# DLRM tower: the first chunk's x rows made by transposes instead of a trip through DRAM

## What is computed

```python
e = stack([tbl_f[ids[:, f]] for f in range(32)], axis=1)     # (B=512, F=32, D=32) fp32
x0 = prev = e
for W in (filter_0, filter_1):                               # (F*32, 128), (F*128, 128)
    z = einsum('bhd,bmd->bhmd', x0, prev)                    # all products of a field and a previous row
    cur = relu(einsum('bpd,pn->bnd', z.reshape(B, -1, D), W))
    outs.append(cur); prev = cur
z = concatenate(outs, axis=1).sum(-1)                        # (B, 256)
h = relu(concatenate([z, dense_ctx], 1) @ W_top1 + b_top1)
h = relu(h @ W_top2 + b_top2)
y = h @ W_top3                                               # (B, 1)
```

## Time and profile before

| | us |
|---|---|
| median of 3 runs | 919.02 (917.8 to 921.05) |
| the profiled execution | 922.03 |
| its span | 920.0 |
| TensorE matmuls busy in the span | 840.2 (91%) |
| VectorE busy | 747.0 (81%) |
| ScalarE busy | 763.2 (83%) |
| GpSimd busy | 677.8 (74%) |

### The profile page before, as it was taken

How to read it: one execution, slowest core, us unless ns; L and a number is a source line. 1 busy time by engine, 2 the same in 40 slices (tenths; PEclk the granted TensorE clock), 3 DMA queues, 4 the chain that set the end, 5 groups by cost and what they waited for, 6 DMA issues and landing times.

```text
span 920.0 us, 14382 instructions
## 1 busy us (share of the span) xinstructions
PE 840.2 (91%) x3572; PEld 668.7 (73%) x3572; DVE 747.0 (81%) x2380; ACT 763.2 (83%) x2568; POOL 677.8 (74%) x650
## 2 busy tenths in 40 slices
PE   0316999999999999999999999999999999999988
PEld 0113787787888788887887888877888888888753
DVE  0223688898998988988998999988999999999891
ACT  1314999999999899999998999999999999999842
POOL 6772778888888898888888888876676666667550
PEclk9999999999999999999999999999999999999998
DMA  9144666666767666767766677667667766764430
GB/s 268 16 116 128 164 156 153 145 159 161 176 157 163 146 147 160 166 145 173 170 152 145 157 166 153 151 153 169 157 152 166 161 152 153 162 148 94 90 69 0
DMA packets 57718, 133.84 MB, mean 145 GB/s; under 512 B 8785, under 2 KB 22321, under 8 KB 57538
## 3 DMA queue, kind: packets, MB, share of 16 engines
q0 software_dynamic: 22528, 69.22, 41.4%
q1 hardware_dynamic: 32178, 59.94, 20.0%
q10 hardware_dynamic: 2928, 3.76, 1.4%
HBM read 62.64 MB, written 5.24 MB: 74 GB/s over the span
## 4 chain that ended last, share of the span: by engine, by line
PE 53%; DMA 13%; issue 10%; DVE 9%; POOL 9%; ACT 4%; another core or an unknown queue 1%; POOLq 0%; DVEq 0%; ACTq 0%
DMA scaled<-scaled 13%; PE ya L652 9%; PE ya L654 9%; PE ya L653 8%; PE yd L654 6%; PE yd L653 6%; PE yd L652 6%; DVE acc L574 5%; ACT scaled L444 3%; POOL quarter L314 3%; POOL quarter L310 2%; PE acc L652 2%; PE acc L654 2%; PE acc L653 2%; POOL part L318 2%
## 5 line engine op out<-in xcount | busy, mean ns | idle before, releaser
L444 ACT ACTIVATE scaled<-ya,emb 128x128 f32<-128x128 f32 x2304 | 659.7, 384 | 63.4 <-PE ya L654 55.7
L574 DVE SCALAR_TENSOR_TENSOR acc<-yd,emb,acc 128x128 f32<-128x128 f32 x1408 | 395.5, 343 | 7.5 <-PE yd L654 7.5
L310 POOL TENSOR_TENSOR quarter<-scaled 128x512 f32<-128x512 f32 x128 | 197.8, 1545 | 81.5 <-DMA scaled<-scaled 69.6
L652 PE MATMUL ya<-w_hi,prev_hi 128*128 128x512 f32 x576 | 227.3, 395 | 10.3 <-DVE prev_lo L540 5.5
L653 PE MATMUL ya<-w_lo,prev_hi 128*128 128x512 f32 x576 | 225.2, 391 | 0.0
L654 PE MATMUL ya<-w_hi,prev_lo 128*128 128x512 f32 x576 | 225.0, 391 | 0.0
L652 PE MATMUL yd<-w_hi,prev_hi 128*128 128x512 f32 x448 | 175.2, 391 | 1.8 <-DVE pooled_b L593 1.5
L654 PE MATMUL yd<-w_hi,prev_lo 128*128 128x512 f32 x448 | 174.4, 389 | 0.0
L653 PE MATMUL yd<-w_lo,prev_hi 128*128 128x512 f32 x448 | 174.4, 389 | 0.0
L303 POOL DMA_DIRECT2D scaled<-scaled x128 | 119.0, 930 | 73.6 <-ACT scaled L444 69.0
L287 POOL DMA_INDIRECT emb<-in_tbl,idx x128 | 132.8, 1038 | 30.3 <-issue 27.2
(11 more groups left out here) (68 smaller groups left out, 723.7 us busy)
## 6 DMA issues: line engine op xcount, KB each, us to landing
scaled<-scaled POOLq DMA_DIRECT2D x128, 512.0 KB
xb<-xt_scratch SPq DMA_DIRECT2D x64, 512.0 KB
x<-xt_scratch SPq DMA_DIRECT2D x64, 192.0 KB
xm<-xt_scratch SPq DMA_DIRECT2D x32, 256.0 KB
emb<-in_tbl,idx POOLq DMA_INDIRECT x128, 4.2
scaled<-in_L_rec_filter SPq DMA_DIRECT2D x8, 256.0 KB
xt_scratch<-xt_stage SPq DMA_DIRECT2D x7, 256.0 KB
xt_scratch<-xt_stage SPq DMA_DIRECT2D x9, 128.0 KB
```

The source lines that it names most:

```text
L310: pool.tensor_tensor(four, piece[:, 0:C], piece[:, C:2 * C], ALU.add).then_inc(quartered, 1)
L444: op = act.activation(scaled[:, tile % PR, C * j + N * i:C * j + N * (i + 1)], ya[:, n % RA, N * i:N * (i + 1)], ACT.Copy, scale=scale_of( ...
L574: dve.scalar_tensor_tensor(after, y_part, scale_of(tile, HB * j + i), before, ALU.mult, ALU.add).then_inc(chained, 1)
L652: pe.matmul(dst, v_hi, m_hi, start=start, stop=False)
```

## The change

For chunk 0 the loads from the scratch, the split products and the small product go. ScalarE repeats each field four times (repeat_four_times), VectorE lays the fields out in four steps (spread_up, nine copies). TensorE transposes these into PSUM: the x that everything is multiplied by, its rows once, and five sets of rows, 28 transposes in seven groups. ScalarE copies two of them to SBUF, VectorE makes five products, and TensorE multiplies them whole in fp32 with the unsplit filter (five matmuls), in place of 13 fp32r ones. Ahead of it stand 34 matmuls whose result is not used (WARM), behind the first 24 gathers. Loads begin at chunk 1; the first write takes columns of chunks 1 to 3, and the second write goes ahead of the first load. The steps of chunk 1's layer 0 move to later places in chunk 0 on ScalarE, TensorE and GpSimd, and EARLY_NEXT goes from 22 to 12. Waits that count chunks are shifted by one; those lines are left out here.

```diff
-    EARLY_NEXT = 22
+    EARLY_NEXT = 12
+    WARM = 34
...
+        fields_up = sb("fields_up", [P, DC, 4 * (F + 4)])
+        fields_four_times = sb("fields_four_times", [P, DC, 4 * F])
...
+        first_product = scaled_flat[:, (F + 2 * KT + 2) * N:(F + 2 * KT + 2) * N + (KT + 1) * C].rearrange(
+            "p (t c) -> p t c", t=KT + 1)
+        first_x = scaled_flat[:, 8192:8192 + C]
+        first_x_once = scaled_flat[0:F, 8192 + C:8192 + 2 * C]
...
+        first_rows = [yd[:, 0, :], yd[:, 1, :], yd[:, 2, :], prod[:], xm_ps[:]]
+        FIRST_TURN = (2, 4, 5, 6, 7)
...
+        def first_emb(fields):
+
+            return emb[:, 0, D * fields.start:D * fields.stop].rearrange("b (f d) -> b d f", d=D)[:, 0:DC]
...
             sp.wait_ge(a_used, 1)
-            write_xt(0, 0, 2, xt_first_written)
+            write_xt(0, 1, 4, xt_first_written)
+            sp.wait_ge(a_used, 2)
+            write_xt(0, 4, CPB)
             sp.wait_ge(xt_first_written, 32)
-            load_l0(0)
             load_l0(1)
-            sp.wait_ge(a_used, 2)
-            write_xt(0, 2, 4)
-            write_xt(0, 4, CPB)
-            sp.wait_ge(xt_written, 64)
-            for c in range(2, CHUNKS):
+            load_l0(2)
+            sp.wait_ge(xt_written, 32)
+            for c in range(3, CHUNKS):
...
-            small_product(1)
             for c in range(CHUNKS):
-                if c + 1 < CHUNKS:
+                if 0 < c < CHUNKS - 1:
...
-                    if q == 1 and c + 2 < CHUNKS:
+                    if c == 0 and q == 1:
+                        small_product(1)
+                    if c == 0 and q == 2:
+                        small_low(1)
+                    if c + 2 < CHUNKS and q == (3 if c == 0 else 1):
...
+            def repeat_four_times(fields):
+                once = first_emb(fields)
+                act.activation(fields_four_times[:, :, 4 * fields.start:4 * fields.stop].rearrange("b d (f i) -> b d f i", i=4),
+                               bass.AP(once.tensor, once.offset, [list(dim) for dim in once.ap] + [[0, 4]]),
+                               ACT.Copy).then_inc(four_times_ready, 1)
+
             act.wait_ge(gathered_first, 16 * EARLY)
+            repeat_four_times(slice(0, EARLY))
             sort_d(0, slice(0, EARLY))
             act.wait_ge(gathered[0], 16 * (F - EARLY))
+            repeat_four_times(slice(EARLY, F))
             sort_d(0, slice(EARLY, F))
+            act.wait_ge(first_turned, 1)
+            act.activation(first_x, xm_ps[:], ACT.Copy).then_inc(first_x_copied, 1)
+            act.wait_ge(first_turned, 3)
+            act.activation(first_x_once, acc0[0:F], ACT.Copy).then_inc(first_x_copied, 1)
             stage_xt(0, 0)
             stage_xt(0, 1)
-            copy_xm(0)
-            split_high(0, 0)
-            small_high(0)
-            for k in range(1, KT):
-                split_high(0, k)
             prev_high(0)
...
+                        if c == 0:
+                            if (q, j) == (1, 1):
                                 copy_xm(1)
-                            if j == 1:
+                            if (q, j) == (1, 3):
                                 split_high(1, 0)
-                            if j == 2:
+                            if (q, j) == (2, 0):
                                 split_high(1, 1)
-                            if j == 3:
+                            if (q, j) == (2, 1):
+                                split_high(1, 2)
+                            if (q, j) == (2, 2):
                                 small_high(1)
-                        elif j == 0 and (q < 3 and c + 1 < CHUNKS):
-                            split_high(c + 1, q + 1)
-                        if j == 0 and (q == 3 and c + 2 < CHUNKS):
-                            split_high(c + 2, 0)
-                        if (q, j) == (3, 1) and c + 1 < CHUNKS:
-                            prev_high(c + 1)
-                        if c + 2 < CHUNKS:
-                            if (q, j) == (2, 2):
-                                copy_xm(c + 2)
-                            if (q, j) == (3, 3):
-                                small_high(c + 2)
+                            if (q, j) == (2, 3):
+                                split_high(1, 3)
+                            if (q, j) == (3, 1):
+                                copy_xm(2)
+                            if (q, j) == (3, 2):
+                                split_high(2, 0)
+                            if (q, j) == (3, 4):
+                                prev_high(1)
+                                small_high(2)
...
+            def spread_up(i, fields, at):
+
+                dve.tensor_copy(fields_up[:, :, 4 * at + i:4 * (at + fields.stop - fields.start - 1) + i + 1:4],
+                                first_emb(fields)).then_inc(fields_up_ready, 1)
+
+            def spread_up_last():
+                n = F - EARLY
+                last = first_emb(slice(EARLY, F))
+                to = fields_up[:]
+                dve.tensor_copy(bass.AP(to.tensor, 4 * (EARLY - 12) + 3, [list(to.ap[0]), list(to.ap[1]), [15, 4], [4, n]]),
+                                bass.AP(last.tensor, last.offset, [list(last.ap[0]), list(last.ap[1]), [0, 4], list(last.ap[2])])
+                                ).then_inc(fields_up_ready, 1)
+
+            def multiply_first(t):
+                if t == 0:
+                    dve.wait_ge(first_x_copied, 1)
+                if t == KT:
+                    dve.wait_ge(first_x_copied, 2)
+                dve.wait_ge(first_turned, FIRST_TURN[t])
+                if t < KT:
+                    product = dve.tensor_tensor(first_product[:, t, :], first_rows[t], first_x, ALU.mult)
+                else:
+                    product = dve.tensor_tensor(first_product[0:F, t, :], first_rows[t][0:F], first_x_once, ALU.mult)
+                product.then_inc(first_multiplied, 1)
...
-            product(0, 0)
-            first_small()
-            for k in range(KT):
-                split_low(0, k)
-                if k + 1 < KT:
-                    product(0, k + 1)
+            dve.wait_ge(gathered_first, 16 * EARLY)
+            for i in range(4):
+                spread_up(i, slice(4 * i, EARLY), 0)
+                spread_up(i, slice(0, 4 * i + 4), F - 4 * i)
+            dve.wait_ge(gathered[0], 16 * (F - EARLY))
+            spread_up_last()
+            for t in range(KT + 1):
+                multiply_first(t)
             prev_low(0)
...
+            def turn_first(dst, source, columns):
+                rows = len(range(*columns.indices(source.shape[2])))
+                for d in range(DC):
+                    turn = pe.transpose(dst[0:rows, P * d:P * (d + 1)], source[:, d, columns], identity[:])
+                turn.then_inc(first_turned, 1)
...
+            pe.wait_ge(ctx_share_ready, H1 // P)
+            pe.wait_ge(w_lo_ready, 4)
+            pe.wait_ge(gathered_first, 16 * EARLY)
+            for _ in range(WARM):
+                pe.matmul(yd[:, 0, :], w1_hi[:, 0, :], w1_hi[:, 0:HB, :], start=True, stop=True)
+            pe.wait_ge(four_times_ready, 2)
+            turn_first(xm_ps[:], fields_four_times, slice(0, P))
+            pe.wait_ge(fields_up_ready, 9)
+            turn_first(first_rows[0], fields_up, slice(0, P))
+            turn_first(acc0[:], fields_four_times, slice(0, P, 4))
+            for t in range(1, KT):
+                turn_first(first_rows[t], fields_up, slice(4 * t, 4 * t + P))
+            pe.wait_ge(first_x_copied, 2)
+            turn_first(first_rows[KT], fields_up, slice(19, 4 * (F + 4), 4))
             pe.wait_ge(sorted_d, 2)
             turn_x(0, 0)
-            turn_x(0, 1)
-            pe.wait_ge(w_lo_ready, 2)
-            for k in range(KT):
-                layer0(0, k)
-            layer0_rest(0)
-            pe.wait_ge(w_lo_ready, 4)
-            pe.wait_ge(ctx_share_ready, H1 // P)
+            for t in range(KT):
+                pe.wait_ge(first_multiplied, t + 1)
+                if t == 1:
+                    turn_x(0, 1)
+                pe.matmul(acc0[:], w0_a[:, t, :], first_product[:, t, :], start=t == 0, stop=False)
+            pe.wait_ge(first_multiplied, KT + 1)
+            pe.matmul(acc0[:], w16[0:F], first_product[0:F, KT, :], start=False, stop=True).then_inc(l0_done, 1)
...
+                        if (c, q, j) == (0, 2, 2):
+                            layer0(1, 1)
+                        if (c, q, j) == (0, 3, 1):
+                            layer0(1, 3)
+                            layer0_rest(1)
+                    if (c, q) == (0, 1):
                         layer0(1, 0)
-                    if q < 3 and c + 1 < CHUNKS:
+                    if (c, q) == (0, 2):
+                        layer0(1, 2)
+                    if c > 0 and q < 3 and c + 1 < CHUNKS:
```

76 lines of the change are left out of this document (43 added, 33 removed).

## The result

| | before | changed |
|---|---|---|
| median, us | 918.61 (917.8 to 921.05, 4 runs) | 926.06 (925.73 to 926.36, 4 runs) |
| the profiled execution, its span | 922.03, 920.0 | 925.75, 923.9 |
| TensorE, VectorE, ScalarE, GpSimd busy | 840.2, 747.0, 763.2, 677.8 | 856.0, 745.5, 763.9, 682.3 |

The changed kernel takes 1.0076 of the time of before, 95% interval 1.0054 to 1.0098: slower by 7.4 us.

What follows compares the result with a forecast made beforehand. TensorE was taken to bound the loop (24.8 us a chunk), leaving gain only where it idles, at the start. -22.0 + 9.1 - 0.5 + 10.2 + 2.2 = -1.0: profiled 922.0 to 921.0, less 3.0 gives 918.0; range 912 to 923.

Steps and rivals of the forecast that it cites:

- The start: Up to TensorE's first bank: moves from 80.05 to 58.0 us, a gain of 22.0 (bounds 17 and 24).
- It stands 3.0 above the median, so the forecast is 918.0: Last step of the sum: the profiled 922.0 would become 921.0, less 3.0 to get from profile to median.
- Chunk 0: First chunk: waits for small products on TensorE and ScalarE give back 9.1 us (bounds 5 and 12).
- Chunks 2 to 4: Loop: 75.0 us in place of 75.5, 0.5 gained (bounds 1.1 gained, 2 lost).
- Chunk 5: Sort of batch tile 1: ScalarE waits 10.5 us for a gather in tile 19's slot; 10.2 lost, at least 3.
- The later gathers: Chunks 6 to 16: four more tiles with a gather make GpSimd lag; 2.2 us lost (bounds 0 and 4.3).
- the gathers come in time: Rival, chance 0.26: GpSimd reaches tile 19's slot early, ScalarE waits 0 to 3 us; 908 to 911 us.
- The clock falls during the transposes: Rival, chance 0.16: 28 transposes at the start leave TensorE at the low clock, costing 5.5 us; 923.5 us.
- Chunk 0 is other than walked: Rival, chance 0.08: halvings collide with chunk 1's loads, 922 to 925 us; or small product doesn't hold ScalarE, 905.

Runs made afterwards that it cites:

- run 7: The changed kernel with VectorE's eight copies of the first 24 fields moved behind the last gather of batch tile 0; 942.70 us in one execution.
- Run 2: The kernel before with EARLY_NEXT = 12 in place of 22, nothing else; 933.80 us, 1.0169 of before.
- run 3: The changed kernel with chunk 0's GpSimd order altered, the small product of chunk 1 ahead of the first sum; 916.13 us, 0.9966 of before.
- run 1: The changed kernel with EARLY_NEXT = 14 in place of 12, two gathers more ahead of the loop; 913.61 us, 0.9935 of before.
- Run 6: run 5 with the gathers of a chunk's first three tiles, from chunk 1 on, issued behind its first halving, ahead of the sum; 917.94 us, 0.9943 of before.
- run 5: The changed kernel with the edits of run 1 and run 3 together; 926.28 us, 1.0031 of before.
- run 4: The changed kernel without the 34 filler matmuls (WARM = 0); 925.97 us, 1.0075 of before.
- run 9: The changed kernel once more, no edit, on a third chip; 940.61 us, 1.0188 of before.

## Why the prediction was wrong

The forecast was 918.0 with a range up to 923; the result is 926.06 and lies outside. The mechanism of the forecast was right, an early start that is given back half in chunk 0 and half at chunk 5. The sum failed at one step and at two sizes: of the 8.1 us between forecast and result, 3.0 are the step from the profile to the median, 2.8 the term of chunk 0 and 1.8 that of the later gathers. The other terms nearly cancel (0.5).

- **The start** (-22.0): -21.3 measured. Walked to 58.0, it came at 58.76; the gathers land 1.7 later, of which 0.9 are the gather beside the copies (run 7), for which the sum had 0.3, and the chain behind the landing took 10.46 where 11.1 were walked (46.56 to 57.7). But the 80.05 that it was measured against had a hole in it. Run 2 shows the same chain without one, first bank 76.51. Against that the start gains 17.8. Since the 22.0 and the -21.3 are both counted from 80.05, the hole is not in the miss of this term; it comes in with the next step.
- **"It stands 3.0 above the median, so the forecast is 918.0"**: this is the step that failed. The profiled execution of before is 3.4 above the median of before, that of the change 0.3 below its own. The excess belonged to before's execution, not to both. If the excess sits in the stretch that the change replaces, a sum of differences made against that execution already holds it, and to subtract it once more gives the gain twice. Without that step the forecast is 921 and the top of its range 926, which is where the result lies. That the excess is the hole of 3.9 us is likely and not shown: the profiled 922.03 is none of the four timed runs of before (917.8 to 921.05), it is like the medians of the three groups with holes (921.80 to 922.42), and in the group without, before took 919.57; but no profile of before from a group without holes was taken.
- **Chunk 0** (+9.1): +11.9, at the top of its bounds (12). The walk was right up to layer0_rest(1), 85.72 for the 85.5 predicted; what failed is the stretch behind it, where layer0_rest(2) came at 115.33 for 111.7. The walk left out what the wait of 4.88 us does to the clock: the matmuls behind it take 0.63 in place of 0.39, granted clock 0.74, and ScalarE waits for them. From 85.72 to 91.43 there are 13 of them; at 0.2275 each they would take 3.0 us and not 5.7, so an estimate of 2.7 us for this stretch. In run 3 the wait is gone and the clock is 0.91, but the second wait (3.40) has gone with it, so the share of the clock alone isn't shown.
- **Chunks 2 to 4** (-0.5): -1.3, just beyond its bound of 1.1. A chunk takes 24.73 us here, where the floor was put at 24.8.
- **Chunk 5** (+10.2): +10.4, though by other parts. ScalarE was at its sort at 198.6 and the slot started 2.0 later, not the 4.0 of the earlier trace rows, since GpSimd lagged less; the gather landed in 6.2, not 6.5. So the wait was 8.22 in place of 10.5, but behind it the clock was low (0.77 from 210 to 220 us), which the walk left out and which about made up for it. That the size came out is luck. Runs 1 and 2 show the term on either kernel: 27.16 with 14 gathers, 38.68 with 12.
- **The later gathers** (+2.2): +4.0, in the bounds. Both parts of the term were too small: run 1, which has no long wait, takes 7.5 us more than before over these chunks (385.6 against 378.1) where 4.2 were walked, and the wait gave back 3.5 of it where 2.0 were walked. Run 6 against run 5 shows that GpSimd's order is what bounds these chunks (8.7 us).

The sum of the terms, with 0.2 behind layer0_rest(21), is +3.9 for the predicted -1.0; the double subtraction is the other 3.0.

Of the rivals, "the gathers come in time" is refuted by the wait of 8.22 us and by run 1. "The clock falls during the transposes" is refuted by the rows at 48.66 and 53.51, and its price by run 4. It forecast 923.5, near the time by accident. "Chunk 0 is other than walked" named 922 to 925 and the right chunk, but not the cause: the first halving's sum came 7.7 us after it, sooner than the 8.4 of the walk. On the Trainium skill's sentence (TensorE: Matmul & The Clock Gate, Part 4: PE-mode transpose) that a transpose doesn't count as busy for the clock, run 4 speaks against it: between 47.75 and 53.66 TensorE did 28 transposes of this kernel, after 15.17 idle us, and nothing else, and the length of four fell from 1.06 to 0.60.

What stays open is how the hole arises. Shown is that ScalarE and VectorE resume 3 to 20 us late on counts that TensorE raises, that the same kernel has it in one group and not in another, that in the new start it ends some 4 us after the last gather, and that it is gone from the start when GpSimd issues no gathers there. Whether the counts or TensorE itself are late can't be told from these rows, since the ends of matmuls are modelled.

## What to carry to other kernels

A profiled execution is one sample: look in the chain for idle time that no instruction of the kernel ends, and don't both count it in a difference and subtract the profile's excess over the median. Where a walk leaves TensorE waiting, as here for 4.88 and 8.00 us, price the low clock behind the wait too. When work is moved out of the start, ask first which slot of the loop its last needed piece lands in; here two gathers more ahead of the loop were worth 6 to 12.5 us (6.1 by profiles, 8.2 and 12.5 by medians). And when a start hangs on short hand-overs between engines, keep GpSimd's gathers away from it: holding them back by 7 us brought the first bank from 76.5 to 57.5 and, between two groups, 9 to 11 us, and with the order of run 6 it made the fastest kernel, 908.08. What the wait costs where there is no hole was not run.

## What was not expected of the hardware

- The same kernel differs by 14.5 us (926.06 and 940.61) and by 18.8 us (913.61 and 932.43) between groups of runs, each on another chip, while before differs by 3 (919.57 to 922.42). It arises at the start, beside gathers of 0.94 us each: the first bank of the change at 58.76 and at 76.48. In the hole little moves: in run 9, from 47 to 66 us, the DMA engines are busy 6%.
- While TensorE waited 4.88 us in chunk 0 and 8.00 us at chunk 5, its level fell, and the first matmuls after it took 0.63 where they take 0.39.
- 34 filler matmuls, 9.39 us of TensorE, changed the level that the transposes start at and brought the first bank 2.9 us closer to the landing. In the profiles the end comes 6.2 us earlier with them, though run 4's was the slowest of its runs; in the medians nothing is seen (926.06 and 925.97). So what they are worth at the end is not settled.
